# A depthwise convolution moved from VectorE to GpSimd, its Silu set behind the decays on ScalarE, and a sum of key squares set ahead of a projection on TensorE

## The reference

```python
qk = x @ qk_w.T ; vg = x @ vg_w.T
q = silu(causal depthwise convolution of q, 4 taps)     # 128 features
k = silu(the same of k)                                 # 128 features
v = silu(the same of v)                                 # 256 features
beta = sigmoid(x @ b_w.T + ...) * 2
g = -exp(A_log) * softplus(x @ a_w.T + dt_bias)         # exp(g) is the decay
q = q * rsqrt(sum of q*q per head) * DK**-0.5 ; k = k * rsqrt(sum of k*k per head)
# per step: S = S*exp(g); delta = (v - k S)*beta; S = S + k delta; o = q S
```

## Time and profile before

| | |
|---|---|
| profiled execution | 831.77 us, span 829.9 us |
| three runs | 832.76, 833.2, 840.58 us; median 833.2 |
| TensorE (PE) busy | 762.5 us, 92% of the span |
| VectorE (DVE) busy | 538.8 us, 65% |
| ScalarE (ACT) busy | 265.2 us, 32% |
| GpSimd (POOL) busy | 215.6 us, 26% |

### The profile page before, as it was taken

One profiled execution on the slowest core, in us unless ns is written; L12 is line 12 of the kernel. 1 busy time (PEld: TensorE's weight loads), 2 busy tenths in 40 slices (PEclk: granted clock), 3 DMA queues, 4 the chain that ended last, 5 costly groups with the idle time before them and its releaser, 6 DMA issues. The chain is left out here.

```text
span 829.9 us, 11442 instructions
## 1 busy us (share of the span) xinstructions
PE 762.5 (92%) x3982; PEld 560.9 (68%) x3982; DVE 538.8 (65%) x1312; ACT 265.2 (32%) x414; POOL 215.6 (26%) x187
## 2 busy tenths in 40 slices
PE   5899999989999999999999498998957999999995
PEld 4422333477788888887456387777734999999985
DVE  4599996458555544455799999998666443434336
ACT  2455778343334434343571111121231000000000
POOL 4470000032223222231030000976002344444410
PEclk9989999979999999999999799999976999999997
DMA  8695000110111111140022405200015899999953
GB/s 293 154 210 96 2 2 3 39 39 20 58 38 57 38 57 38 57 153 1 25 90 77 190 1 171 59 1 1 1 51 189 310 351 344 335 347 346 337 191 109
DMA packets 38516, 101.17 MB, mean 122 GB/s; under 512 B 5294, under 2 KB 18278, under 8 KB 37510
## 3 DMA queue, kind: packets, MB, share of 16 engines
q1 hardware_dynamic: 34470, 91.06, 33.9%
q0 software_dynamic: 3552, 9.11, 2.9%
q10 hardware_dynamic: 448, 0.39, 0.2%
HBM read 84.17 MB, written 16.57 MB: 121 GB/s over the span
## 5 line engine op out<-in xcount | busy, mean ns | idle before, releaser
L1332 PE MATMUL psum<-xr,wr 128*128 128x512 f32 x600 | 145.9, 393 | 1.0 <-DVE arena L1969 1.0
L1332 PEld LDWEIGHTS psum<-xr,wr 128*128 128x128 f32 x600 | 113.9, 190 | 25.4 <-issue 1.7
L720 POOL TENSOR_TENSOR wr<-ring,wr 128x512 fp32r<-128x512 f32 (+1 forms) x50 | 55.0, 1120 | 257.2 <-ACT wr L888 257.2
L1645 PEld LDWEIGHTS psum<-arena 128*128 128x128 f32 x700 | 85.2, 195 | 3.4 <-issue 1.7
L1819 DVE TENSOR_REDUCE small<-psum 128x1 f32<-128x512 f32 x128 | 80.9, 685 | 9.3 <-PE psum L1211 8.4
L1645 PE MATMUL psum<-arena 128*128 128x128 f32 x700 | 85.6, 278 | 1.1 <-issue 0.6
L1655 PE MATMUL psum<-arena 128*128 128x256 f32 x350 | 81.4, 380 | 0.2 <-issue 0.2
L2425 DVE TENSOR_SCALAR arena<-psum,arena 128x256 f32<-128x256 f32 x35 | 16.9, 484 | 98.3 <-PE psum L1655 98.3
L1343 PE MATMUL psum<-hr,wr 128*128 128x512 f32 x300 | 76.6, 391 | 0.9 <-DVE hr L1906 0.9
L1932 DVE TENSOR_TENSOR hid<-hid,psum 128x512 f32<-128x512 f32 x50 | 34.4, 688 | 59.9 <-ACT hid L894 59.7
L867 ACT ACTIVATE arena<-psum 128x1024 f32<-128x1024 f32 x64 | 63.0, 1024 | 27.2 <-PE psum L1221 26.4
(11 more groups left out here) (379 smaller groups left out, 1213.3 us busy)
## 6 DMA issues: line engine op xcount, KB each, us to landing
arena<-in_w1u SPq DMA_DIRECT2D x35, 642.5 KB
arena<-in_w1d SPq DMA_DIRECT2D x35, 640.0 KB
ring<-in_w SPq DMA_DIRECT2D x25, 384.0 KB, 3.0
part_scratch<-arena SPq DMA_DIRECT2D x12, 256.0 KB, 4.3
z_scratch<-w_a SPq DMA_DIRECT2D x4, 768.0 KB, 7.2
arena<-z_scratch SPq DMA_DIRECT2D x8, 384.0 KB, 6.5
arena<-part_scratch SPq DMA_DIRECT2D x9, 256.0 KB, 7.7
qkv_scratch<-arena SPq DMA_DIRECT2D x4, 512.0 KB, 2.7
```

Source lines behind the costliest of these rows:

```text
L720: pool.tensor_tensor(wr0[:, k, LO, part], ring0[:, k, part], wr0[:, k, HI, part], ALU.subtract).then_inc(s["w0_lo"], 1)
L1332: ins = pe.matmul(bank[2 * b + m][:, :], wr0[:, k, w, lo:lo + P], xr[:, x, f, half(b)], start=(f == 0 and (w, x) == PARTS[0]), stop=(f == ...
L1645: ins = pe.matmul(bank[2 + r % 2 * 3 + k // 2][:, tile(k % 2)], wup1[:, r % NW, lo:lo + P], xgT[:, r % 2, f, :], start=(f == 0), stop=(f = ...
```

## The change

- The queries' convolution leaves VectorE. GpSimd does it, between clearing `Di` and the products of the decays, in seven instructions of 128x1024: four `tensor_scalar` (one per tap) and three `tensor_tensor` adds, waiting for the copies of the query chunk and for the keys' convolution.
- On ScalarE the Silu of the queries moves from between the copies to behind the last Exp of the decays, ahead of `root(1)`.
- On TensorE `norm_sum(0)` moves from between the two batches of the last projection to ahead of both.
- On VectorE `proj_out(2)` moves ahead of the decays' arguments.

```diff
@@ GpSimd
             ch.link(pool.memset(Di, 1.0))
+            pool.wait_ge(s["proj_act"], 2)
+            pool.wait_ge(s["proj_dve"], 2)
+            pool.wait_ge(s["conv"], 1)
+            acc = co[:, CHUNKS[1], :].rearrange("p (b n) -> p b n", b=B)
+            tap_out = [x.rearrange("p (b n) -> p b n", b=B) for x in (R16[:, 0:TOK], R16[:, TOK:2 * TOK], Sall[:, TOK:2 * TOK])]
+
+            def tap_of(to, tap):
+                w = CONVW + CHUNKS[1] * CONV + tap
+                return pool.tensor_scalar(to, cin[:, CHUNKS[1], :, tap:tap + S], cols[:, w:w + 1], None, ALU.mult)
+
+            ch.link(tap_of(acc, CONV - 1))
+            for tap in range(CONV - 2, -1, -1):
+                formed = ch.mark(tap_of(tap_out[tap], tap))
+                if tap == CONV - 2:
+                    ch.need(formed)
+            for tap in range(CONV - 2, -1, -1):
+                ins = pool.tensor_tensor(acc, acc, tap_out[tap], ALU.add)
+                if tap:
+                    ch.link(ins)
+            ins.then_inc(s["conv"], 1)
@@ ScalarE
             for n, m in enumerate(CHUNKS):
-                if n >= 2:
-                    conv_silu(n - 2)
+                if n == 2:
+                    conv_silu(0)
...
             act.activation(g_(5), g_(5), ACT.Exp, scale=-1.0).then_inc(s["d_act"], 1)
+            conv_silu(1)
             root(1, q2, "q_to")
@@ TensorE
-                    if pos == 6 and b:
+                    if pos == 6 and b == 0:
                         norm_sum(0)
@@ VectorE
-            for n, m in enumerate(CHUNKS[:2]):
-                proj_out(m)
-                dve.wait_ge(s["proj_act"], n + 1)
-                dve.wait_ge(s["proj_dve"], n + 1)
-                conv(dve, ch, m)
+            proj_out(CHUNKS[0])
+            dve.wait_ge(s["proj_act"], 1)
+            dve.wait_ge(s["proj_dve"], 1)
+            conv(dve, ch, CHUNKS[0])
+            proj_out(CHUNKS[1])
...
+            proj_out(2)
             dve.wait_ge(s["ab_in"], 16)
...
-            proj_out(2)
             proj_out(3)
```

## The result

The changed kernel is slower: 844.76 us median of four runs (842.3 to 846.99) against 835.77 us of the kernel before on the same chip (the three runs above and one of 838.33), a ratio of 1.0115 with a 95% interval of 1.0074 to 1.0155, or some 10 us. The profiled execution took 844.97 us with a span of 842.8. That is 12.9 us more span than the profiled execution before. The stretch of the change, from the first projection to the copy behind the last pair sum, took 58.42 us before (401.44 to 459.86) and takes 70.74 now (402.91 to 473.65): **12.3 us more**. So I compare the length of this stretch.

A forecast was written before the change was run, and what follows sets the result against it. It took TensorE's chain from `norm_sum(1)` to the last pair sum as the bound; 5.7 (later Silu) + 1.6 (clock) = 7.3 us on 831.77 gave 839.1, stated as 839.8 after half the median's offset, range 834 to 848.

The forecast's parts named there:

- likeliest case: Queries return late and TensorE is late with them, GpSimd's work covered: 836.5 to 842 us, chance 0.60.
- GpSimd is late: GpSimd's seven take up to 25.9 us, outlasting 14.4 us of cover; Silu up to 11.4 us later, 850.5 us; chance 0.25.
- What bounds the stretch: Before 460 us, TensorE's last pair sum decides, VectorE 0.33 us ahead; lateness at `norm_sum(1)` carries to the end.
- VectorE's 4.63 us count as nothing: Freeing VectorE of the queries' convolution, 4.63 us, only puts it further ahead of TensorE: counted as nothing.
- faster rival: VectorE's relief counts because the queries return before 430: 827 to 831.5 us, chance 0.05.
- Moving the sum of key squares costs nothing: `norm_sum(0)` ahead of both blocks of the last projection is the same TensorE work in another order: no cost.
- The Silu's place: Queries' Silu behind the Exp on ScalarE makes `norm_sum(1)` 5.5 us late and the pair sums 5.7 us late.
- The clock: TensorE waits some 5.4 us ahead of `norm_sum(1)`, its clock falls to the lower level: +1.6 us, range 0 to 3.
- GpSimd's seven: GpSimd's convolution takes 12.5 us from 413.1, ending at 425.6, covered until the Silu's table is ready at 427.55: cost 0.
- Contention: Shared memory interfaces let VectorE slow GpSimd's convolution, at 3.7 us per 1024-wide instruction; within a rival of chance 0.25.
- The delay is swallowed: Later work waits for something that doesn't move, shrinking the 7 us to 0 to 3: 832 to 835, chance 0.10.
- The added table load: On ScalarE the moved Silu needs another load, 1.28 us, with no drain; by the skill page 1.4 us more.

The follow-up runs named there:

- kernel before with GpSimd loaded: Kernel before plus seven GpSimd instructions (four tensor_scalar, three adds) whose results nobody reads, VectorE still convolving: 842.91 us against 834.78, ratio 1.0125.
- one-tap run: Changed kernel with GpSimd's seven instructions cut to the first, the other three taps and the adds left out: 845.61 us against 834.78, ratio 1.014.
- run with one tap and TensorE kept busy: Changed kernel with GpSimd cut to one product and 23 extra matmuls ahead of `norm_sum(1)`: 840.75 us against 836.29, ratio 1.0065.

## Why the prediction was right and where it was not

The direction, the place and the range held: slower, by a late sum of the queries' squares, 844.76 us within 834 to 848. The likeliest case did not happen whole. It had GpSimd covered; the rival "GpSimd is late", at 0.25, is what came, with 3.6 to 3.9 of the up to 11.4 us that it was given. Of the chances, too, the smaller one came: I gave 0.60 to a change within 1% and 0.38 to slower by more; measured is 1.15%, though its interval, 0.74 to 1.55%, reaches to both sides. That the range held is in part luck, since its upper end was made for a GpSimd slowed by VectorE, and something else filled it. The terms add up to 12.3 us in the stretch where the sum had 7.3; the missing 5.0 are 3.6 of GpSimd, 1.15 of the clock and 0.3 of the order.

- **What bounds the stretch**: right. TensorE's rigid chain from `norm_sum(1)` on passes any lateness to the last pair sum. In every run ScalarE waits 7.16 us for it, and from the pair sums' start to their end the time is the same. Only in the kernel before with GpSimd loaded does VectorE end later still.
- **VectorE's 4.63 us count as nothing**: right. It waits 2.57 us at its second reciprocal and again at the pair sums. The faster rival falls with it.
- **Moving the sum of key squares costs nothing**: right for the whole change (0.20 us of waiting, and the Silu 1.27 us sooner than with the Silu moved alone), wrong if taken as a statement on the move by itself (1.55).
- **The Silu's place, +5.7**: right; 5.98 measured with the other two terms taken away. The way from the Silu through memory took 6.67 us where I had 6.84.
- **The clock, +1.6**: the fall came, its size was too small: 2.4 to 2.75. I had taken the restart of the earlier trace rows with 3.1 us at half speed; this one stood there for about 5, the one of the one-tap run, behind a pause of 5.37 us, for about 5.7. Another restart in the trace before, at 621.49, would have given a better size: its clock stood at 0.50 until about 627.5.
- **GpSimd's seven, cost 0**: this step failed. I bounded `tensor_scalar` between a memset and an add and took 1.5 us; it is 2.85, above the bound of 2.12. At this shape the instruction that reads one tensor and a scalar per partition costs GpSimd more than the one that reads two tensors. The adds took 2.35 instead of 2.12. So 18.7 us instead of 12.5, against a cover of 14.4. The Silu starts as the last add ends, 3.88 us later than with one tap; the 0.74 us that the Exp waits for VectorE lie within that time and add nothing to it. What held is the rival's rule, that GpSimd decides one for one as soon as its seven exceed their cover.
- **Contention**: I held the late rival's mechanism to be GpSimd slowed by VectorE. It is mostly the other way round: `tensor_scalar` takes 2.85 us with VectorE idle and 2.85 in the changed kernel. It takes 3.0 beside VectorE's normalization and, in the loaded kernel, 3.36 beside VectorE's convolution, while VectorE's own small instructions grow severalfold. The 924 ns from which I priced the rival are for the most part the price of the small shape: the first of those four products took 0.86 us, ahead of VectorE's products, which began at 570.80, and the last, beside them, 1.11. The Trainium skill, "GPSIMD Engine Reference", Key points, says that the two share interfaces and contend when VectorE reads two inputs or runs in a two-port mode. The runs agree for two inputs and show who pays most: a 128x128 `tensor_tensor` of 0.29 us became 2.32. So did a `tensor_scalar`; whether that one runs in a two-port mode no run shows.
- **"The delay is swallowed"**: no sign of it; from the copy behind the last pair sum to the end it is 370.0 us before and 369.2 after.
- **The added table load**: in the run with one tap and TensorE kept busy, where the Silu waits for nothing else, the added load starts at 427.96, 0.02 us behind the Exp, and the Silu follows its end within 0.02 us. So the sum without a drain was the right one.

The measured 1.15% is a few microseconds under the profiled stretch's 12.3; the interval, 6.2 to 13.0 us, holds both that and the forecast's 7.3.

## What to carry to other kernels

Before an instruction is moved behind another on its engine, follow what its result sets off: here one Silu of 1.06 us opened a way of two transfers, a square and a sum, with 2.1 us of slack on it, and losing its place cost 6 us with no work added but a table load of 1.28. Taking work from an engine that is a third of a microsecond ahead of another gains nothing; look first at who is waited for at the end of the stretch. When work goes to an idle engine, price its instructions there by a run of the very form, and price what they do to VectorE beside them.

## What the runs showed of the hardware that I had not expected

GpSimd's `tensor_scalar` with a scalar per partition, 128x1024 in float32, takes 2.84 us with VectorE nearly idle and up to 3.36 beside VectorE's convolution; its add of two tensors takes 2.34 to 2.44. While an add runs, a VectorE instruction of 128x128 can last as long as the add (2.32 us instead of 0.29), with one or two tensor inputs alike; in the changed kernel two reciprocals of 128x128 beside the same adds kept their 0.95 us. After a pause of 9.3 us TensorE's clock stayed at the lower level for some 5 us of continuous work, in other restarts of these traces for 3 to 6.
